# Dealing a kernel's first filter work anew between two engines, and giving its output rows four places in place of two

## The chip, the cores and the metric

The kernel runs on one core of one Trainium2 chip. The metric is the device time of one execution in microseconds (us), lower is better. TensorE does matrix products and transposes, VectorE (DVE), ScalarE (ACT) and GpSimd (POOL) work elementwise, SyncE (SP) asks for transfers, and 16 DMA engines carry them. SP, ACT and POOL each have a queue in which their requests for transfers stand among their other instructions.

## The reference, cut to what matters

Everything is float32. N = 128 samples, C = 32 channels, L = 512 positions.

```python
# block 0
h = conv1d(x, conv_w, 9 taps, pad 4, 4 channel groups of 8)      # (N, 32, 512)
h = h + (cond @ ctx_w.T)[:, :, None] + fside[None, :, None]
top2 = top_k(h @ W_gate + b_gate, 2)                              # 8 experts, per row of 512
x = x + mean over the two chosen experts of relu(h @ W_e + b_e)
# block 1
att = softmax(mlp(cond)); agg_w = att @ mix_w; agg_b = att @ mix_b   # per sample a 32x32 mix
y = agg_w @ x + agg_b
x = x + (y @ dequant(qweight, scales, zeros) + bias)
```

## The kernel before, in words

A group is 4 samples with 32 channels, that is 128 rows of 512; there are NG = 32 groups. The program has three stages, each engine's order is written out by hand, and semaphores tie them.

*Stage 1, convolution and routing (to about 145 us).* The convolution is computed on four interleaved phases of the positions (position = 4 l + q). `split_phase` (L387) copies phase q of a group from the loaded x (32 channels on 32 partitions) to the partitions of `phases`. For each group TensorE does 12 products against the filter `wconv` (L1281), ACT brings the result to `hT` (L598), and gating and ranks follow. For group 0 something must come first: the filter. The weights `conv_w` come in four transfers, one for each channel group, into a zeroed square `wfull`; `pick_taps` (L377) copies 12 shifted pieces of it to `wsel`, three steps t of four pieces p; TensorE turns each step's four pieces (L1205), and DVE copies each step's result to `wconv` (L764). DVE takes two pieces of each step, ACT the other two. ACT asks for two of the four weight transfers and for `bg_bc`, loads its table at its first copy (L589), takes its pieces, and only then copies phases 3 and half of 2 of group 0. DVE takes its pieces, then phases 0 and 1, then the filter copies, then the other half of phase 2. TensorE runs 24 transposes of `ident` ahead of all this (`warm_up`, L1197), whose results nobody reads, and after the filter transposes two small ones for the condition (L1209, L1210), which await `cond_sb` and `cw_sb` from SP's queue.

*Stage 2, expert products (to about 385 us).* 71 blocks of 128 rows are gathered, multiplied by their expert's weights (L1307), and scattered.

*Stage 3, mixing and the last linear layer (from about 385 us).* SP's `load_group(a)` brings x and the pair of expert results of group a; POOL adds (L578), DVE finishes y (L1124, `finish_y`). TensorE goes by pairs of groups a, a+1: `mix_group` (L1351) and `sum_terms` (L1358) of both, `add_terms` of a-1 (L1380), `linear` of both, first with the `high` part (L1368), then the `low` part (L1372), then `add_terms` of a. ACT makes `high` (L711) and `token_rows` (L705), DVE makes `low` (L1108) and scales (L1096, `scale_bank`); `add_terms(c)` waits for `scale_bank(c)`. DVE's `out_row(d)` (L1118) adds y to the finished bank into one of two places `orow[:, d % 2]`, and for that waits until the store of row d-2 has landed (`out_out[d % 2]`). ACT asks for that store in `store_row(d)` (L716), which waits for `out_row(d)`; what stands behind it on ACT waits too. `ring_a` is two tiles of 128x512 that stage 2 uses between DVE and ACT and stage 3 does not.

## Time and profile before

| | us |
|---|---|
| median of 3 runs | 491.54 |
| lowest, highest | 491.21, 492.26 |
| profiled execution, its own time | 496.68 |
| its span in the trace | 494.9 |
| TensorE busy in the span | 480.5 |
| mean granted TensorE clock | 0.992 |

The profiled execution is one of its own and is 5.14 us above the median of the timed ones; 1.8 us of it lie outside the span. The trace gives for each instruction a start, a duration, and what its engine last waited for. A granted clock of 1.00 stands for 2.4 GHz, 0.50 for 1.2 GHz.

### The profile page before, as it was taken

How to read it: one execution, taken by the hardware profiler on the slowest of the kernel's cores; microseconds unless marked ns; L12 is line 12 of the kernel's file. 1: busy time of each engine (PE TensorE's matmuls, PEld its weight loads, DVE VectorE, ACT ScalarE, POOL GpSimd, SP SyncE). 2: the span in 40 equal slices, each digit the busy share in tenths (PEclk: the TensorE clock that was granted, in tenths of full speed). 3: DMA queues.
4: the chain of work that ended last, by engine and by line, in shares of the span. 5: the costliest groups of instructions: out<-in, count | busy, mean ns of one | idle time of the engine just before them, and what ended most of it. 6: DMA issues, size and time to landing. Idle time of an engine off the chain costs nothing.

```text
span 494.9 us, 10081 instructions
## 1 busy us (share of the span) xinstructions
PE 480.5 (97%) x2341; PEld 324.7 (66%) x2342; DVE 323.8 (65%) x966; ACT 176.8 (36%) x309; POOL 196.9 (40%) x215
## 2 busy tenths in 40 slices
PE   7999999999999999999999999999999989999996
PEld 6999999998964444444444444444445667888885
DVE  5688778988747567564354535344356688888885
ACT  5587878898721211111212112112222212211221
POOL 8055555654637532332332323323224434334420
PEclk8899999999999999999999999999999999999999
DMA  6799978998976875777656657576657599999812
GB/s 169 214 330 291 306 235 303 299 295 237 285 195 204 228 220 139 183 219 206 198 154 165 189 151 206 139 201 159 194 151 198 168 368 353 319 312 313 299 72 101
DMA packets 90052, 110.95 MB, mean 224 GB/s; under 512 B 25199, under 2 KB 61727, under 8 KB 88981
## 3 DMA queue, kind: packets, MB, share of 16 engines
q1 hardware_dynamic: 66912, 59.70, 44.4%
q0 software_dynamic: 11952, 37.28, 21.0%
q10 hardware_dynamic: 11144, 13.48, 8.1%
q8 instruction: 16, 0.26, 0.2%
q14 instruction: 28, 0.22, 0.1%
HBM read 65.44 MB, written 46.51 MB: 226 GB/s over the span
## 4 chain that ended last, share of the span: by engine, by line
PE 78%; DVE 9%; issue 4%; DMA 3%; SPq 2%; ACT 1%; DVEq 1%; ACTq 1%; another core or an unknown queue 0%
PE bank L1307 40%; PE bank L1281 14%; PE bank L1268 7%; PE bank L1351 4%; PE bank L1368 4%; PE bank L1372 4%; DMA out<-orow_list 3%; PE bank L1380 2%; PE bank L1358 1%; SPq L454 1%; DVE ring_a L1000 1%; DMA keys<-lists_d 1%; DVE bank L1096 1%; DVE orow_list L1118 1%; DVE phases L387 1%
## 5 line engine op out<-in xcount | busy, mean ns | idle before, releaser
L1307 PE MATMUL bank<-we,lT 128*128 x536 | 232.3, 594 | 0.6 <-DVE ring_a L1000 0.6
L1307 PEld LDWEIGHTS bank<-we,lT 128*128 128x128 f32 x536 | 101.1, 190 | 127.2 <-issue 126.9
L562 POOL DMA_INDIRECT pairs_d<-ring_b,pair_i x71 | 71.5, 1007 | 150.6 <-DVE pair_i L989 99.2
L658 ACT ACTIVATE ring_b<-ring_a 128x512 f32<-128x512 f32 x71 | 44.7, 630 | 191.2 <-DVE ring_a L1000 182.9
L1000 DVE TENSOR_TENSOR ring_a<-bank,be_bc 128x512 f32<-128x512 f32 x71 | 49.1, 692 | 96.9 <-PE bank L1307 50.3
L543 POOL DMA_INDIRECT lists_d<-token_list,row_i x64 | 69.3, 1083 | 72.4 <-issue 33.6
L1281 PE MATMUL bank<-wconv,phases 128*128 128x128 f32 x768 | 93.8, 280 | 0.8 <-ACT phases L387 0.8
L1281 PEld LDWEIGHTS bank<-wconv,phases 128*128 128x128 f32 x768 | 90.8, 196 | 1.7 <-ACT phases L387 1.0
L387 DVE COPY phases<-xt 32x512 f32<-32x512 f32 (+1 forms) x96 | 52.5, 547 | 9.2 <-PE bank L1281 6.0
L387 ACT COPY phases<-xt 32x512 f32<-32x512 f32 x64 | 56.4, 882 | 1.5
L578 POOL TENSOR_TENSOR we<-xt,we 128x512 f32<-128x512 f32 x26 | 33.5, 1291 | 55.7 <-DVE we L1124 49.7
L986 DVE STREAM_TRANSPOSE lT<-xt 128x512 f32<-128x512 f32 x67 | 47.2, 704 | 9.8 <-DMA keys<-lists_d 9.1
L711 ACT CAST high<-bank 128x512 fp32r<-128x512 f32 x32 | 18.6, 584 | 75.9 <-PE bank L1351 72.2
L1268 PE MATMUL bank<-wg,lT 128*128 128x136 f32 x256 | 37.4, 289 | 0.4 <-ACT token_list L622 0.4
L1372 PE MATMUL bank<-wq,low 128*128 128x512 f32 x128 | 35.0, 395 | 1.0 <-DVE low L1108 0.9
L1368 PE MATMUL bank<-wq,high 128*128 128x512 f32 x128 | 35.3, 398 | 0.0
L1268 PEld LDWEIGHTS bank<-wg,lT 128*128 128x128 f32 x256 | 31.8, 190 | 1.3 <-issue 1.2
L1096 DVE TENSOR_TENSOR bank<-bank,scale_bc 128x512 f32<-128x512 f32 x32 | 22.3, 697 | 10.7 <-PE bank L1372 10.5
L1372 PEld LDWEIGHTS bank<-wq,low 128*128 128x128 f32 x128 | 23.8, 188 | 7.7 <-DVE low L1108 2.3
L1368 PEld LDWEIGHTS bank<-wq,high 128*128 128x128 f32 x128 | 24.1, 189 | 5.0 <-issue 0.2
L1351 PEld LDWEIGHTS bank<-mix_bd,we 128*128 128x128 f32 x208 | 25.2, 192 | 1.2 <-DVE we L1124 0.3
L598 ACT COPY lT<-bank 128x512 f32<-128x512 f32 x32 | 18.7, 584 | 20.0 <-PE bank L1281 13.6
(212 smaller groups left out, 379.8 us busy)
## 6 DMA issues: line engine op xcount, KB each, us to landing
xt<-lists_d SPq DMA_DIRECT2D x268, 64.0 KB
xt<-in_x SPq DMA_DIRECT2D x58, 256.0 KB, 4.7
we<-pairs_d SPq DMA_DIRECT2D x26, 512.0 KB, 5.7
we<-in_L_ffn_W_e SPq DMA_DIRECT2D x8, 1024.0 KB
out<-orow_list ACTq DMA_DIRECT2D x32, 256.0 KB, 4.6
words<-pairs_d POOLq DMA_DIRECT2D x6, 512.0 KB, 5.3
lists_d<-orow_list SPq DMA_DIRECT2D x8, 257.0 KB
be_bc<-in_L_ffn_b_e ACTq DMA_DIRECT2D x4, 512.0 KB
```

Source lines behind the costliest of these rows:

```text
L387: return copy(phases[q * C:(q + 1) * C, jb, samples, 1:P + 1], x_quad[jq].rearrange("c s (l q) -> c q s l", q=PH)[:, q, samples, :])
L543: pool.indirect_dma_start(lists_d, bass.IndirectOffsetOnAxis(ap=row_i[:, j, k:k + 1], axis=0), token_list[:, j, :], None, bounds_check=E * ...
L562: pool.indirect_dma_start(pairs_d, bass.IndirectOffsetOnAxis(ap=pair_i[:, s % DR:s % DR + 1], axis=0), ring_b[:, s % U, :], None, bounds_c ...
L658: act.activation(ring_b[:, j, :], ring_a[:, j % 2, :], ACT.Relu, scale=0.5).then_inc(result_ready, 1)
L986: dve.transpose(lT[:, ja, :].rearrange("m (p h r) -> m h p r", p=PH, h=MH), list_of(a, ja).rearrange("r (h p l) -> r h p l", h=MH, p=PH)). ...
L1000: dve.tensor_tensor(ring_a[:, j % 2, :], ps_exp[j % 2][:, :], be_bc[:, bass.ds(expert, 1), :].rearrange("p a n -> p (a n)"), ALU.add).then ...
L1268: mm = pe.matmul(gate_out[:, p, 0:E + P], hT[:, ja % 2, p * P:(p + 1) * P], wg[:, p, :], start=True, stop=True)
L1281: mm = pe.matmul(ps_conv[j % 2][:, s * P:(s + 1) * P], phases[:, j % 2, s, t:t + P], wconv[:, t, :, :].rearrange("k p o -> k (p o)"), star ...
L1307: mm = pe.matmul(ps_exp[j % 2][:, :], lT[:, j, p * P:(p + 1) * P], we[:, bass.ds(expert, 1), p, :].rearrange("m a n -> m (a n)"), start=(p ...
L1351: mm = pe.matmul(ps_mix[a % 2][:, q * P:(q + 1) * P], y_of(a)[:, q * P:(q + 1) * P], mix_bd[:, a, :], start=True, stop=True)
L1368: pe.matmul(ps_lin[j][:, :], high[:, j % 2, q * P:(q + 1) * P], wq[:, q, :], start=(q == 0), stop=False, skip_group_check=True)
L1372: mm = pe.matmul(ps_lin[j][:, :], low[:, j % 2, q * P:(q + 1) * P], wq[:, q, :], start=False, stop=(q == PH - 1), skip_group_check=True)
```

## The change

Three edits.

1. *Start.* SP asks for three weight transfers in place of two, ACT for one; `bg_bc` is asked for after ACT's pieces. DVE takes 8 pieces and ACT 4. DVE copies phases 0 and 1 of group 0 ahead of its pieces and the whole of phase 2 behind them; ACT copies phase 3 ahead of its pieces and nothing of phase 2.
2. *TensorE.* 20 transposes of `warm_up` in place of 24, and 2 behind each step of filter transposes.
3. *End.* `row_ring` has four places, two in `orow` and the two tiles of `ring_a`; `out_row(d)` waits for the store of row d-4. ACT asks for the store of an odd row one step later, between the next pair's two `high_part`.

```diff
+        row_ring = [orow[:, 0, :], orow[:, 1, :], ring_a[:, 0, :], ring_a[:, 1, :]]
...
-        out_out = [sem(f"out_out{i}") for i in range(2)]
+        out_out = [sem(f"out_out{i}") for i in range(U)]
...
+        taps_of_dve = [range(3), range(3), range(2)]
+        taps_of_act = [range(3, PH), range(3, PH), range(2, PH)]
...
-            for s in range(2):
+            for s in range(3):
...
-            for s in range(2, C // CG):
-                rows = slice(s * CG, (s + 1) * CG)
-                act.dma_start(wfull[rows, rows, PH - 1:PH - 1 + TAPS], conv_w[rows]).then_inc(convw_in, 16)
-            act.dma_start(bg_bc[:, :], b_gate.rearrange("(a e) -> a e", a=1).to_broadcast((P, E))).then_inc(bg_in, 16)
+            rows = slice(3 * CG, 4 * CG)
+            act.dma_start(wfull[rows, rows, PH - 1:PH - 1 + TAPS], conv_w[rows]).then_inc(convw_in, 16)
             act.wait_ge(ident_ready, 2)
             act.copy(g0[:, 0:1], ident[:, 0:1])
+            act.wait_ge(pads_ready, 2)
+            act.wait_ge(x_in[0], 16)
+            split_phase(act.copy, 3, 0, 0).then_inc(act_split, 1)
             act.wait_ge(convw_in, 16 * (C // CG))
-            pick_taps(act.copy, range(PH // 2, PH), act_taps)
+            pick_taps(act.copy, taps_of_act, act_taps)
+            act.dma_start(bg_bc[:, :], b_gate.rearrange("(a e) -> a e", a=1).to_broadcast((P, E))).then_inc(bg_in, 16)
...
-                act.dma_start(out_g[g], orow[:, g % 2, :]).then_inc(out_out[g % 2], 16)
+                act.dma_start(out_g[g], row_ring[g % U]).then_inc(out_out[g % U], 16)
...
                 if a > 2:
                     high_part(a)
+                    store_row(a - 3)
                 high_part(a + 1)
                 store_row(a - 2)
                 if a > 2:
                     high_sums(a)
                 high_sums(a + 1)
-                store_row(a - 1)
+            store_row(NG - 3)
...
+            split_x(0, 0)
             dve.wait_ge(convw_in, 16 * (C // CG))
-            pick_taps(dve.tensor_copy, range(PH // 2), dve_taps)
-            split_x(0, 0)
+            pick_taps(dve.tensor_copy, taps_of_dve, dve_taps)
+            split_phase(dve.tensor_copy, 2, 0, 0).then_inc(dve_split, 1)
...
-            split_third(0)
...
-                wait(dve, out_out[d % 2], (d - d % 2) * 8)
-                dve.tensor_tensor(orow[:, d % 2, :], ps_lin[d % U][:, :], y_of(d), ALU.add).then_inc(out_ready, 1)
+                wait(dve, out_out[d % U], (d - d % U) * (16 // U))
+                if d in (2, 3):
+                    dve.wait_ge(result_ready, NT)
+                dve.tensor_tensor(row_ring[d % U], ps_lin[d % U][:, :], y_of(d), ALU.add).then_inc(out_ready, 1)
...
-            warm_up(3 * WARM_START)
+            warm_up(5 * WARM_START // 2)
...
                 mm.then_inc(wT_done, 1)
+                warm_up(2)
```

ACT's first instructions before, up to the copies of group 0 (`words` holds both `wfull` and `wsel`):

```order
L586 DMA words<-in_L_cond_weight 8x8x9 [waits wfull_zero]
L586 DMA words<-in_L_cond_weight 8x8x9
L587 DMA bg_bc<-in_L_ffn_b_gate 128x8
L589 ACT_TABLE_LOAD
L589 COPY g<-ident 128x1 [waits ident_ready]
L377 COPY words<-words 32x128 [waits convw_in]
L377 COPY words<-words 32x128 x5
L387 COPY phases<-xt 32x4x128 [waits x_in0,pads_ready]
L387 COPY phases<-xt 32x2x128
```

And ACT's first instructions now:

```order
L589 DMA words<-in_L_cond_weight 8x8x9 [waits wfull_zero]
L591 ACT_TABLE_LOAD
L591 COPY g<-ident 128x1 [waits ident_ready]
L391 COPY phases<-xt 32x4x128 [waits x_in0,pads_ready]
L381 COPY words<-words 32x128 [waits convw_in]
L381 COPY words<-words 32x128 x3
L597 DMA bg_bc<-in_L_ffn_b_gate 128x8
```

Two requests have left the place ahead of the table load, the phase copy has come ahead of the weights' arrival, and two pieces and the half copy of phase 2 are gone.

DVE's first instructions behind its memset before:

```order
L377 COPY words<-words 32x128 [waits convw_in]
L377 COPY words<-words 32x128 x5
L387 COPY phases<-xt 32x4x128 [waits x_in0]
L387 COPY phases<-xt 32x4x128
L764 COPY wconv<-bank 128x128 [waits wT_done] x3
L387 COPY phases<-xt 32x2x128
```

And the same stretch of DVE now:

```order
L391 COPY phases<-xt 32x4x128 [waits x_in0]
L391 COPY phases<-xt 32x4x128
L381 COPY words<-words 32x128 [waits convw_in]
L381 COPY words<-words 32x128 x7
L391 COPY phases<-xt 32x4x128
L772 COPY wconv<-bank 128x128 [waits wT_done] x3
```

Two phase copies stand ahead of the wait for the weights, and the last one is whole and stands ahead of the filter copies.

ACT in stage 3, from the `high` part of group 3 on, before (L716 is a store):

```order
L711 CAST high<-bank 128x512 [waits lin_done,mixed_done]
L716 DMA out<-orow_list 128x512 [waits out_ready]
L705 CAST rows_r<-bank 34x128 [waits terms_done]
L716 DMA out<-orow_list 128x512 [waits out_ready]
L711 CAST high<-bank 128x512 [waits lin_done,mixed_done] x2
L716 DMA out<-orow_list 128x512 [waits out_ready]
L705 CAST rows_r<-bank 34x128 [waits terms_done] x2
L716 DMA out<-orow_list 128x512 [waits out_ready]
```

The same place on ACT now (L722 is a store):

```order
L717 CAST high<-bank 128x512 [waits lin_done,mixed_done]
L722 DMA out<-orow_list 128x512 [waits out_ready]
L711 CAST rows_r<-bank 34x128 [waits terms_done]
L717 CAST high<-bank 128x512 [waits lin_done,mixed_done]
L722 DMA out<-orow_list 128x512 [waits out_ready]
L717 CAST high<-bank 128x512 [waits lin_done,mixed_done]
L722 DMA out<-ring_a 128x512 [waits out_ready]
L711 CAST rows_r<-bank 34x128 [waits terms_done] x2
```

The store of row 1 stood ahead of the `high` part of group 4 and stands behind it now; rows 2 and 3 of each four leave from `ring_a`.

## Rows read from the trace of the kernel before

**Rows 1.** The page: busy time by engine, and the chain that ended last.
```profile
PE 480.5 (97%) x2341; PEld 324.7 (66%) x2342; DVE 323.8 (65%) x966; ACT 176.8 (36%) x309; POOL 196.9 (40%) x215
...
PE 78%; DVE 9%; issue 4%; DMA 3%; SPq 2%; ACT 1%; DVEq 1%; ACTq 1%; another core or an unknown queue 0%
```

**Rows 2.** The chain that ended last, 0 to 40 us: start, duration, what.
```profile
4.28 1.28 ACT L589
...
5.67 2.01 ACT words L377 x6
...
7.70 1.11 ACT phases L387
...
8.82 0.64 ACT phases L387
...
9.51 5.49 PE bank L1281 x24
...
16.39 2.78 PE bank L1281 x24
```

**Rows 3.** Instructions in order of time, 0 to 30 us: start, duration, instruction.
```profile
3.57 0.43 SPq L401 DMA_DIRECT2D cw_sb<-in_L_cond_c_weight  x1
...
5.26 1.47 DVE L377 COPY words<-words 32x128 f32<-32x128 f32 x6 [3.85 <-DMA words<-in_L_cond_weight]
...
5.58 1.82 SPq L405 DMA_DIRECT2D fs_col<-in_fside_S  x4
...
6.34 1.59 DVE L387 COPY phases<-xt 32x512 f32<-32x512 f32 x2
...
8.15 0.33 PE L1209 MATMUL bank<-ident,cond_sb 128*128 128x128 f32 x1
```

**Rows 4.** Line L1197, to 5.4 us and from 5.5 us: durations in ns, starts.
```profile
L1197 PE MATMUL bank<-ident x18: 357/421/477, 1.6 to 5.3; 128*128 128x128 f32 x18
...
L1197 PE MATMUL bank<-ident x7: 272/273/357, 5.3 to 6.0; 128*128 128x128 f32 x7
```

**Rows 5.** Busy time by stretch; behind the engines clock, DMA share, GB/s.
```profile
5.43:8.86 3.43, 2.49 (x22) 1.84 (x20) 3.37 (x12) 3.38 (x10) 3.43 (x12) 1.00 0.80 201
8.86:15.64 6.78, 6.13 (x29) 6.13 (x29) 2.77 (x7) 2.93 (x4) 3.66 (x7) 0.50 1.05 296
...
397.90:401.30 3.40, 1.69 (x8) 1.07 (x6) 1.55 (x3) 0.00 (x0) 0.00 (x0) 1.00 1.05 413
...
396.00:404.00 8.00, 5.83 (x32) 4.54 (x33) 5.70 (x13) 1.21 (x4) 2.31 (x3) 1.00 1.02 400
```

**Rows 6.** The chain that ended last, from 330 us on.
```profile
393.28 6.38 DMA out<-orow_list
...
423.37 1.78 PE bank L1351 x16
...
430.08 1.78 PE bank L1351 x16
```

**Rows 7.** Instructions in order of time, 372 to 424 us.
```profile
391.64 2.22 PE L1351 MATMUL bank<-mix_bd,phases 128*128 128x128 f32 x16
...
393.73 1.07 ACT L711 CAST high<-bank 128x512 fp32r<-128x512 f32 x2 [3.69 <-DVE orow_list L1118]
...
395.08 0.69 DVE L1118 TENSOR_TENSOR orow_list<-bank,token_list 128x512 f32<-128x512 f32 x1 [1.23 <-DMA out<-orow_list]
...
396.43 1.19 PE L1372 MATMUL bank<-wq,low 128*128 128x512 f32 x4 [0.66 <-DVE low L1108]
...
399.75 0.69 DVE L1118 TENSOR_TENSOR orow_list<-bank,token_list 128x512 f32<-128x512 f32 x1 [2.26 <-DMA out<-orow_list]
...
401.20 0.47 PE L1380 MATMUL bank<-terms_w,rows_r 70*128 70x512 f32 x1 [1.71 <-DVE bank L1096]
...
401.71 2.05 PE L1351 MATMUL bank<-mix_bd,we 128*128 128x128 f32 x16
...
423.20 1.05 PE L1351 MATMUL bank<-mix_bd,we 128*128 128x128 f32 x8
```

More of the change, by code:

```diff
@@ L370, in x_count @@
             return 16 * ((a - PRIMED) // XR + 1)
+        taps_of_dve = [range(3), range(3), range(2)]
+        taps_of_act = [range(3, PH), range(3, PH), range(2, PH)]
         def pick_taps(copy, phases_of, taps_ready):
             for t in range(SHIFTS):
-                for p in phases_of:
+                for p in phases_of[t]:
                     k0 = PH * t - p + PH - 1
@@ L489, in _ @@
             for s in out_out:
-                sp.wait_ge(s, 16 * (NG // 2))
+                sp.wait_ge(s, 16 * (NG // U))
         @block.gpsimd
@@ L600, in step1 @@
                 a = g + 2
-                if live(a, NG):
+                first = isinstance(g, int) and a == 0
+                if live(a, NG) and not first:
                     ja = (j + 2) % U
@@ L625, in step1 @@
                 a = g + 2
-                if live(a, NG):
+                if live(a, NG) and not first:
                     split_phase(act.copy, 2, (j + 2) % U, j % 2, for_act).then_inc(act_split, 1)
@@ L644, in step1 @@
                         act.activation(att_x[:, :], att[:, :], ACT.Exp, accum_out=att_s[:, 0:1]).then_inc(mlp_ev, 1)
-            act.wait_ge(pads_ready, 2)
             stepped(act, step1, -2, lo1, hi1, NG + 2)
```

## The prediction

> **What bounds the kernel now.** I read the page first: TensorE is busy 97% of the span and holds 78% of the chain that ended last [rows 1]. So only two kinds of change can pay: what shortens the time before TensorE's first useful product, or what takes away a stretch in which it waits or runs slowly. The chain in order of time shows where these are.
>
> At the start the chain runs along ACT: its table load, its six filter pieces, the copies of phase 3 and half of phase 2, and then the first convolution at 9.51 [rows 2]. That convolution takes 5.49 us, the next one 2.78 for the same 24 records [rows 2]. The stretches say why: the granted clock is 0.50 from 8.86 to 15.64, with 6.13 us of TensorE work in it, after a stretch in which the engine was busy 2.49 of 3.43 us, and that with small transposes for the most part [rows 5]. At full clock the same work would take half: the low clock costs 6.13 / 2 = 3.07 us. The durations of the warm-up tell one thing more. They fall from 421 to 272 ns at about 5.4 us [rows 4], though the page's clock stands at 1.00 from the start; I take it that TensorE began low, rose 3.85 us after its first transpose (5.43 - 1.58; the warm-up's first start is rounded to 1.6 in the row), fell at 8.86 and rose again at 15.64.
>
> The third stage is bound by TensorE once it has settled: from 423.37 to 430.08 a pair of groups takes 6.71 us [rows 6]. It has not settled at first. The pair that starts at 391.64 takes 10.07 us (to 401.71), and the next three take 21.49 us together (to 423.20) where three settled ones take 20.13 [rows 7]. That is 3.36 + 1.36 = 4.72 us over. The chain names the cause of the larger part: the store of row 1, 6.38 us long [rows 6]. DVE waited 1.23 us for the store of row 0 and 2.26 us for that of row 1; TensorE then waited 0.66 us for the low part and 1.71 us for the scaled bank [rows 7].
>
> **The start, part by part.** *ACT.* Of its two weight transfers one goes, and the one for `bg_bc` moves behind. The table load began at 4.28; it can begin when the first request ends. I put that at 3.05 (the two weight requests together ran from 1.45 to 3.75, and the first of them was the long one), so the load ends at 4.35 instead of 5.56. The phase copy (1.11) then runs from about 4.45 to 5.56. It needs group 0's x. That transfer is asked for first, on the same queue as the weights, which landed at 5.26 [rows 3]; I take it as landed by 4.4. The pieces need the weights, and these come as late as before: the last request leaves SP at about the time when the last left ACT. Four pieces at 2.01 / 6 = 0.335 us end at 6.90. ACT had the last word at 9.46; now it is done at 6.90.
>
> *DVE.* Two phase copies of 0.80 us each (1.59 / 2) [rows 3] fit between x and 5.26 if x has landed by 3.66; if x is late by a, DVE is late by a. Eight pieces at (6.34 - 5.26) / 6 = 0.18 us run to 6.70, the whole copy of phase 2 to 7.50, and only the last filter copy remains, short beside what TensorE does meanwhile.
>
> *TensorE.* Step 0 can be turned at about 6.1 (ACT's first piece ends at 5.97), step 2 after 6.93. Four small transposes take about 0.45 us with their gaps, two fillers at full clock about 0.11 us each, since the warm-up's seven last begin between 5.3 and 6.0 [rows 4]. Steps 0, 1, 2 and their fillers end near 7.8. The condition's two transposes follow. Their data comes from SP behind one more weight request of some 0.7 us: cw_sb was asked for at 3.57 and TensorE got to it at 8.15 without a wait of its own [rows 3]. I put them at 8.0 to 8.5 and the first convolution at 8.5, against 9.51: **1.0 us**. Bounds: 0.4, if the fillers run at low clock (0.21 us each, 6 x 0.1 more) or x makes DVE late by as much; 1.4, if the condition's data is no later than before. The fs_col requests (1.82 us in all) and three loads of x move back by the same 0.7 us; they are covered, since DVE used fs_col at 16.36 and x of group 1 lay there at 9.59. bg_bc is used at 18.0, 11 us after its new place.
>
> *The clock.* Unknown, with bounds 0 and 3.07 us. For a clock that stays up: from 5.43 to 8.86 TensorE would have three warm-ups, six full fillers, the same small transposes and 0.36 us of convolution, some 3.1 of 3.4 us busy; and a stretch of 3.40 us in which the engine was busy only 1.69 us kept 1.00 at 397.90 [rows 5]. Against it: those 1.69 us were large products, most of the new ones are small transposes, and the 2.49 of 3.43 busy at 5.43 did not hold it. I take the clock as kept, 3.0 us, a little nearer to the row at 397.90 than to that at 5.43. The second convolution would start at 8.5 + 6.88 - 3.07 = 12.3 in place of 16.39; its phases need DVE until about 10.8 (two copies for the condition, then 0.6 + 0.6 + 0.4), so nothing new stops it.
>
> The Trainium skill's page "TensorE: Matmul & The Clock Gate", part 1, says of the clock that "the default state is throttled, and activity releases the throttle". The durations at L1197 agree. The advice at the page's end names long idle gaps as what brings the low clock back; the longest gap ahead of the first convolution was under 1 us here and the clock fell all the same, so where page and trace differ the trace decides, and the page alone, which would keep the clock now, is no ground for more than the chance given below.
>
> **The end, part by part.** With four places `out_row(2)` and `out_row(3)` wait for no store, and `out_row(4)` waits for the store of row 0, asked for 10 us earlier; the page gives 4.6 us to landing as the median, and 6.38 is the longest [rows 6]. The store of an odd row, asked for a step later, is awaited a whole pair after that, some 9 us. The new wait for `result_ready` is long met. DVE from 393.16: scale 0.69, out_row(2) to 394.5, low of 4 and 5 (1.28) to 395.8, which needs high of 4. ACT made that at 393.73 because it stood in the store of row 1 [rows 7]; with the store behind it, it is made at about 392.9. Then sums 0.48, out_row(3) to 396.9, scale(4) to 397.6, y of 6 and 7 to 398.9. TensorE has low(4) when it wants it (395.6), scale(4) before 398.4, and begins the next pair at 398.65 in place of 401.71: 3.06 us. The other 1.36 go too if nothing else is late: **4.4 us** in the profiled execution. The ends: 2.4 (0.66 + 1.71 alone) and 4.72. The timed runs are 5.14 us shorter than the profiled one; some of the stores' delay may belong to it alone, so I take **3.9**. The extra request between the two `high` parts costs ACT 0.34 us a pair; ACT idles 5 us a pair. At the very end the last row's store follows its out_row as before: nothing.
>
> **Sum.** 1.0 + 3.0 + 3.9 = 7.9; 491.54 - 7.9 = 483.6.
>
> **Rivals.** *The clock falls, but returns sooner.* The first rise came 3.85 us after the engine got busy; from 8.5 on it is busy without a gap, so a rise near 12.3 is likely where 15.64 was. Low from 8.86 to 12.3 costs 1.7 in place of 3.07: gain 1.4. Sum 1.0 + 1.4 + 3.9 = 6.3: 485.2.
>
> *The clock does as before*, low for 6.78 us from 8.86 with TensorE busy all of it: 3.39 lost, 0.3 more than before. 1.0 - 0.3 + 3.9 = 4.6: 486.9.
>
> *The stores' wait turns into one for loads.* DMA is full between 396 and 404 (share 1.02, 400 GB/s) [rows 5]. If y of 8 to 11 then comes late, TensorE waits where DVE waited, and the tail gives 1.0: 483.6 + 2.9 = 486.5, or 488.1 with the second case of the clock. Against it: a pair needs two loads of 256 KB, two of 512 KB and two stores of 256 KB, 2.1 MB in 6.71 us or 313 GB/s, below the 400 shown. The skill's page "DMA: Bandwidth & Descriptors", in "Issuing engines are not separate DMA queues", says that all requests end on the same 16 engines and interleave: by that alone more stores in flight add no rate, and the tail's gain would be this rival's.
>
> *Slower.* The shorter warm-up ends about 0.4 us after the clock's first rise. Should the rise be missed, and the mix of small transposes and gaps hold it low past the first convolutions, each us of TensorE work costs 0.5 us. It takes 5 us of gain (1.0 - 0.1 + 3.9, about) to be eaten: low for 10 us longer than before, to 25.7. With a low clock to 30 the time would be 493.7. Only one rise is delayed by that, and dense work raised it before; little speaks for it.
>
> **How the numbers follow.** Clock kept 0.42; returns sooner 0.22; as before 0.18; loads in place of stores 0.12; low clock for long 0.06, of which half ends slower. The first gives 483.6, with 482.4 to 485.0 by its own bounds. Range: 482.2 (upper bounds at the start and in the tail) to 487.4 (the third case with a tail of 3.4, and most of the fourth). About 0.2% (1 us) is what a measurement tells from no change: faster 0.94, within it 0.03, slower 0.03.
>
> **What the new profile would show.** The first convolution (now L1291) starts at 8.5 and its 24 records take 2.7 to 2.8 us (kept), or about 5.4 (not), with a clock row of 0.50 only in the latter; ACT ends its pieces by 6.9. DVE's L1127 has no wait for a store. ACT's high of group 4 has no wait for L1127, TensorE's L1390 none of 1.7 us, and pairs follow each other every 6.7 us from the second on. It would be wrong if x of group 0 lands after 5 us, if L1127 or POOL's add waits for transfers in the third stage, or if the clock is low past 12.3.

## The result and the profile after

The changed kernel takes 487.57 us, the median of 7 runs (486.25 to 489.20), against 492.26 for the kernel before, timed beside it (7 runs, 491.21 to 493.15). The ratio is 0.9902, with a 95% interval of 0.9881 to 0.9924: 4.7 us faster, where 7.9 were forecast. The profiled execution took 486.77, with a span of 485.0.

The page of the changed kernel, busy time by engine and the chain that ended last:

```profile
PE 476.7 (98%) x2343; PEld 323.4 (67%) x2344; DVE 324.2 (67%) x968; ACT 175.5 (36%) x306; POOL 197.9 (41%) x215
...
PE 88%; DVE 5%; issue 2%; SPq 2%; DMA 1%; ACT 1%; DVEq 0%; ACTq 0%
```

DMA had 3% of the chain and DVE 9% in [rows 1]; now they have 1% and 5%, and TensorE has 88% where it had 78%. The chain at the start, in order of time:

```profile
4.55 0.82 ACT phases L391
...
5.69 0.42 ACT words L381
...
6.25 0.41 PE bank L1214 x4
6.65 0.37 PE bank L1206 x2
7.02 0.36 PE bank L1214 x4
7.38 0.37 PE bank L1206 x2
7.75 0.36 PE bank L1214 x4
8.11 0.37 PE bank L1206 x2
8.48 0.20 PE bank L1219
...
8.91 4.26 PE bank L1291 x24
...
14.19 2.78 PE bank L1291 x24
```

The part that ran along ACT until 9.5 [rows 2] is gone. TensorE goes from step to step by itself, and its own small work is now what the start consists of: each pair of fillers (L1206) takes 0.37 us of the path. The first convolution starts at 8.91 in place of 9.51 and takes 4.26 in place of 5.49. The clock behind it, in the stretches of [rows 5] (the second cut in two):

```profile
5.43:8.86 3.43, 2.79 (x23) 1.87 (x21) 2.64 (x11) 2.45 (x6) 3.36 (x17) 0.93 0.69 192
8.86:12.27 3.41, 3.41 (x19) 3.41 (x19) 2.09 (x5) 0.88 (x2) 3.41 (x7) 0.57 0.86 215
12.27:15.64 3.37, 3.37 (x33) 3.37 (x32) 2.20 (x6) 2.35 (x3) 0.67 (x2) 1.00 1.03 345
```

It still fell, and came back before 12.27 instead of at 15.64. From the first convolution to the second it is now 5.28 us where it was 6.88, so the clock gave 1.6 us here and not 3.0. That is the rival "the clock falls, but returns sooner", in this execution.

In the third stage, from the timeline:

```profile
387.02 0.59 ACT L717 CAST high<-bank 128x512 fp32r<-128x512 f32 x1 [4.21 <-PE bank L1361]
...
387.32 0.68 DVE L1127 TENSOR_TENSOR ring_a<-bank,token_list 128x512 f32<-128x512 f32 x1
...
389.77 0.69 DVE L1127 TENSOR_TENSOR ring_a<-bank,token_list 128x512 f32<-128x512 f32 x1
...
396.63 1.28 POOL L582 TENSOR_TENSOR we<-xt,we 128x512 f32<-128x512 f32 x1 [2.24 <-DMA we<-pairs_d]
...
399.40 0.47 PE L1390 MATMUL bank<-terms_w,rows_r 70*128 70x512 f32 x1
```

Neither `out_row` carries a wait for a store (1.23 and 2.26 us in [rows 7]), ACT's `high` waits for TensorE alone, and `add_terms` has lost its 1.71 us. POOL does wait for a load, 2.24 us, as the third rival said it might. The chain shows how far apart the pairs start:

```profile
386.10 1.78 PE bank L1361 x16
392.81 1.79 PE bank L1361 x16
399.87 1.78 PE bank L1361 x16
406.77 1.78 PE bank L1361 x16
413.48 1.78 PE bank L1361 x16
```

The pairs follow each other after 6.71, 7.06, 6.90 and 6.71 us. That is 0.35 + 0.19 = 0.54 us over settled pairs. The waits for loads cost at most that here, against the 2.9 that the rival asked for.

### The profile page after: what moved, and what is told of

Its sections match the earlier page's. It is cut to its first block, busy times and chain, and to the rows that moved or that the text cites. A ratio compares the mean times of both kernels' runs of the same rounds, so it can differ in the third digit from the quotient of the medians.

```text
span 485.0 us, 10085 instructions
## 1 busy us (share of the span) xinstructions
PE 476.7 (98%) x2343; PEld 323.4 (67%) x2344; DVE 324.2 (67%) x968; ACT 175.5 (36%) x306; POOL 197.9 (41%) x215
## 4 chain that ended last, share of the span: by engine, by line
PE 88%; DVE 5%; issue 2%; SPq 2%; DMA 1%; ACT 1%; DVEq 0%; ACTq 0%
PE bank L1317 42%; PE bank L1291 16%; PE bank L1378 6%; PE bank L1382 6%; PE bank L1361 6%; PE bank L1278 6%; PE bank L1390 2%; PE bank L1368 2%; SPq L458 1%; DVE phases L391 1%; DMA keys<-lists_d 1%; DVE lT L993 1%; DVE ring_a L1007 0%; ACTq L589 0%; ACT phases L391 0%
## 5 line engine op out<-in xcount | busy, mean ns | idle before, releaser
L1291 PE MATMUL bank<-wconv,phases 128*128 128x128 f32 x768 | 92.7, 278 | 0.0
L1291 PEld LDWEIGHTS bank<-wconv,phases 128*128 128x128 f32 x768 | 89.8, 194 | 0.9 <-issue 0.8
L391 ACT COPY phases<-xt 32x512 f32<-32x512 f32 (+1 forms) x63 | 55.9, 888 | 2.4 <-DMA xt<-in_x 1.0
```

The costliest lines, as they stand in the source:

```text
L391: return copy(phases[q * C:(q + 1) * C, jb, samples, 1:P + 1], x_quad[jq].rearrange("c s (l q) -> c q s l", q=PH)[:, q, samples, :])
L1291: mm = pe.matmul(ps_conv[j % 2][:, s * P:(s + 1) * P], phases[:, j % 2, s, t:t + P], wconv[:, t, :, :].rearrange("k p o -> k (p o)"), star ...
```

## The experiments

There are four sets of runs, each on a chip of its own; every kernel is compared with the kernel before of its set. Times are medians in us. "Clock" counts, of all executions of a kernel, those whose mean granted clock was 0.998 or more, those between, and those of 0.989 or less. At 0.998 or more the clock fell nowhere ahead of the last few us: e12's trace, whose one fall lasted 3.4 us, has 0.996. A lower mean does not say where the clock fell. e11's trace has 0.996 too, but there the clock held at the start and fell at 138 us. So where the text says that so many executions kept the clock, it means 0.998 or more, and counts no execution that kept it at the start and lost it later.

| kernel | time | before in its set | ratio, 95% interval | clock |
|---|---|---|---|---|
| e1 before again | 494.65 | 494.77 | 0.9996 [0.9973, 1.0019] | 0 / 8 / 4 |
| e2 start (edits 1, 2) | 494.55 | 494.77 | 0.9990 [0.9961, 1.0018] | 0 / 10 / 2 |
| e3 end (edit 3) | 489.69 | 494.77 | 0.9877 [0.9839, 0.9915] | 1 / 5 / 0 |
| e4 changed | 488.62 | 494.77 | 0.9877 [0.9844, 0.9910] | 4 / 2 / 0 |
| e5 four places, stores as before | 490.08 | 495.69 | 0.9874 [0.9846, 0.9903] | 2 / 3 / 1 |
| e6 two places, later stores | 510.21 | 495.69 | 1.0292 [1.0261, 1.0324] | 0 / 0 / 6 |
| e7 changed, no fillers | 487.76 | 495.69 | 0.9839 [0.9816, 0.9862] | 5 / 0 / 0 |
| e8 edits 2 and 3 | 488.81 | 495.69 | 0.9860 [0.9837, 0.9884] | 2 / 4 / 1 |
| e9 no fillers, x first | 486.41 | 494.42 | 0.9850 [0.9810, 0.9890] | 4 / 2 / 0 |
| e10 edit 3, x first | 489.96 | 494.42 | 0.9914 [0.9882, 0.9946] | 2 / 4 / 0 |
| e11 as e7 | 488.01 | 494.42 | 0.9870 [0.9829, 0.9910] | 3 / 3 / 0 |
| e12 changed | 488.81 | 494.42 | 0.9894 [0.9861, 0.9926] | 4 / 2 / 0 |
| e13 changed, x first | 488.70 | 495.58 | 0.9864 [0.9837, 0.9890] | 2 / 4 / 0 |
| e14 as e9 | 486.07 | 495.58 | 0.9810 [0.9780, 0.9839] | 5 / 1 / 0 |
| e15 changed | 488.22 | 495.58 | 0.9851 [0.9816, 0.9886] | 3 / 3 / 0 |

Marks from their traces: when the durations of TensorE's first transposes drop (421 to 272 ns for the warm-up's, as in [rows 4]; a drop behind the warm-up is read from the filter's) and whether the clock then fell at the start or was kept; the starts of the first two convolutions and of the first gating product, the time from there to that of the last group, the start of the third stage's first pair, and the next four pairs together (four settled ones take 26.84).

| profiled execution | drop, clock | conv(0) | conv(1) | first gating | to the last | first pair | four pairs | span |
|---|---|---|---|---|---|---|---|---|
| before | 5.4, fell | 9.51 | 16.39 | 19.01 | 122.64 | 391.64 | 31.56 | 494.9 |
| e1 before | 5.0, fell | 9.49 | 16.16 | 18.77 | 120.60 | 389.35 | 31.23 | 492.6 |
| e2 start | 5.1, fell | 8.88 | 14.22 | 16.84 | 121.22 | 387.12 | 32.61 | 491.5 |
| e3 end | 4.9, fell | 9.48 | 16.11 | 18.73 | 120.49 | 389.34 | 27.23 | 488.5 |
| after | 5.0, fell | 8.91 | 14.19 | 16.81 | 119.48 | 385.93 | 27.39 | 485.0 |
| e4 changed | 6.5, kept | 8.87 | 12.76 | 15.38 | 121.42 | 386.44 | 27.21 | 485.6 |
| e12 changed | 5.2, fell | 8.77 | 14.24 | 16.85 | 121.35 | 387.62 | 26.88 | 486.4 |
| e15 changed | 4.4, fell | 9.32 | 15.77 | 18.39 | 120.90 | 388.19 | 27.19 | 487.3 |
| e11 no fillers | 4.6, kept | 8.16 | 12.09 | 14.71 | 123.00 | 387.88 | 26.96 | 486.8 |
| e9 no fillers, x first | 5.8, kept | 8.42 | 12.35 | 14.97 | 121.17 | 385.32 | 27.16 | 484.2 |
| e14 as e9 | 6.6, kept | 8.44 | 12.37 | 14.99 | 121.64 | 385.55 | 26.96 | 484.4 |
| e13 fillers, x first | 6.4, kept | 8.81 | 12.71 | 15.32 | 121.89 | 386.81 | 27.31 | 486.1 |
| e5 four places | 4.7, fell | 9.52 | 16.02 | 18.64 | 121.30 | 391.68 | 27.29 | 490.9 |
| e6 two places, later stores | 5.7, fell | 9.52 | 14.88 | 17.50 | 120.17 | 388.03 | 38.02 | 507.9 |
| e7 no fillers | 4.4, kept | 8.47 | 12.26 | 15.02 | 122.26 | 386.89 | 27.29 | 486.1 |
| e8 edits 2 and 3 | 5.4, fell | 9.51 | 16.38 | 18.99 | 122.10 | 392.61 | 27.22 | 491.8 |
| e10 edit 3, x first | 7.5, kept | 9.50 | 13.46 | 16.08 | 122.31 | 388.46 | 26.85 | 487.0 |

The first column orders most of the outcomes. In the ten traces whose clock fell the durations drop between 4.4 and 5.7 us. In five of the seven that kept it they drop at 5.8 or later, whatever the edits: e10 has the old start. The other two, e7 and e11, drop early and kept it all the same; both run without fillers. What moves the drop from one execution to the next the traces do not show.

### First set: the two halves apart

**e1** is the kernel before without an edit.

> The kernel before, unchanged, to see how its executions differ among themselves and what its spans look like in other profiled executions. Theory A (the recorded execution of 496.68 us was an outlier, and part of its stall at the stores of rows 0 and 1 belongs to it alone): this profile has a span near 490 us, the pair of groups 4 and 5 takes clearly less than 10.07 us, and out_row(0) has no wait of 2.4 us. Theory B (the stall is typical and the gain was lost elsewhere in the changed kernel): a span near 490 us too, but with the pair still at about 10 us and a shorter start or middle.

Its trace differs from the first one by 2.3 us of span (492.6 and 494.9), 2.04 of them between the first and the last gating product. The stall is there too: the pair of groups 4 and 5 takes 10.17 us (389.35 to 399.52) where the first trace had 10.07, and behind it stand the same two waits:

```profile
DVE orow_list L1118 <- DMA out<-orow_list: 3.2, 2, 2.6
...
PE bank L1380 <- DVE bank L1096: 2.1, 1, 2.1
```

So theory B holds, the stall is typical. Over the four sets the kernel before ran 68 times, from 491.94 to 498.23.

**e2** has the start alone:

```diff
-            pick_taps(act.copy, range(PH // 2, PH), act_taps)
+            pick_taps(act.copy, taps_of_act, act_taps)
...
-            warm_up(3 * WARM_START)
+            warm_up(5 * WARM_START // 2)
...
                 mm.then_inc(wT_done, 1)
+                warm_up(2)
```

> Edits 1 and 2 alone (the new deal at the start, the fillers), with the old two places at the end. Theory A: the start is worth what the trace of the changed kernel shows, 2.2 us (16.39 to 14.19 at the second convolution), so 2.2 us faster than before, 1.5 to 3. Theory B: the clock takes most of it back in the median execution, 0.7 us faster. My prediction on record had 4.0.

It measured 494.55, against 494.65 for e1: nothing that can be told from no change, though its profiled execution is 1.94 us ahead of e1's at the second convolution and 2.23 ahead at the first pair. In the third stage it gives 1.38 back, four pairs taking 32.61 us where e1's take 31.23. From its timeline:

```profile
396.05 0.69 DVE L1123 TENSOR_TENSOR orow_list<-bank,token_list 128x512 f32<-128x512 f32 x1 [4.85 <-DMA out<-orow_list]
...
397.49 0.68 PE L1386 MATMUL bank<-terms_w,rows_r 70*128 70x512 f32 x1 [3.73 <-DVE bank L1101]
```

With two places the store of row 0 (7.63 us long here) holds the second pair up just as before. The stall costs more than its length, as the stretches behind it show:

```profile
397.00:398.00 1.00, 0.51 (x2) 0.21 (x2) 1.00 (x4) 0.00 (x0) 0.00 (x0) 0.79 1.02 406
398.00:399.00 1.00, 1.00 (x5) 1.00 (x5) 1.00 (x3) 0.00 (x0) 0.83 (x1) 0.50 1.07 430
```

After 3.73 us without work TensorE's clock was 0.50 from 397.6 to 401, and 3.4 us of its time went at half speed. In [rows 5] the clock had stayed up in a stretch with waits of 1.71 us and less, so I had not counted this. It stayed up behind e1's wait of 2.05 us as well.

**e3** has the end alone:

```diff
-        out_out = [sem(f"out_out{i}") for i in range(2)]
+        out_out = [sem(f"out_out{i}") for i in range(U)]
...
-                wait(dve, out_out[d % 2], (d - d % 2) * 8)
+                wait(dve, out_out[d % U], (d - d % U) * (16 // U))
...
+                    store_row(a - 3)
...
-                store_row(a - 1)
```

> Edit 3 alone (four row places, each odd store a step later), with the old start. Theory A: 2.5 us faster than before, since the typical stall is smaller than the recorded one. Theory B: 3.9 us, as predicted.

5.1 us faster. Four pairs take 27.23 us, 4.00 less than e1's. The rest of the 5.1 may be a second fall of the clock, argued from counts and not shown: of the 68 executions of the kernel before, 31 had a mean clock of 0.989 or less (median 496.03, the others' 494.3), and of the 25 of the changed kernel none had. But neither trace of the kernel before has such a fall, and four places do not rule a second fall out, as e5 and e8 show below.

**e4** is the changed kernel again.

> The changed kernel again, beside its parts on the same chip. Theory A and B: 4.7 us faster than before. If the parts add, e2 and e3 sum to it within 0.7 us.

488.62: the start adds 1.1 us to e3, with intervals that overlap. Here the clock was kept: the first convolution took 2.88 us and the second started at 12.76, 3.35 ahead of e3's. At the end of the span 2.9 of that is left, though between the medians it is 1.1. In the timeline around the seventh group a load of x is late:

```profile
36.05 1.28 DVE L391 COPY phases<-xt 32x512 f32<-32x512 f32 x2 [1.27 <-DMA xt<-in_x]
```

TensorE then stood idle for 1.05 us, until 39.43.

### Second set: what each edit of the halves does

**e5** has the four places, and each store where it stood.

```diff
+        row_ring = [orow[:, 0, :], orow[:, 1, :], ring_a[:, 0, :], ring_a[:, 1, :]]
...
-                wait(dve, out_out[d % 2], (d - d % 2) * 8)
+                wait(dve, out_out[d % U], (d - d % U) * (16 // U))
```

> Half of edit 3 on the kernel before: four row places, but each store asked for where it was. Theory A (the wait for a row place makes the stall): out_row(2) and out_row(3) wait for no store; ACT still stands in the store of row 1, so high of group 4 is made some 0.8 us late and TensorE may wait 0.2 to 0.6 us for the low part. 4.5 us faster than before, the granted clock never at 0.98 to 0.99 for want of a second fall. Theory B (the place of the store request on ACT matters as much): 2 to 3 us faster.

5.6 us faster, as much as e3, and its four pairs take 27.29 us where e3's take 27.23. The later request adds nothing that can be measured. One part of the expectation failed: the profiled execution had a mean clock of 0.988. Its clock fell a second time, but not in the third stage: TensorE waited 1.03 us ahead of the last group's gating products, and from 141.2 to 144.6 us the clock was 0.50.

**e6** is the opposite: two places, and the later request.

```diff
                     high_part(a)
+                    store_row(a - 3)
...
-                store_row(a - 1)
+            store_row(NG - 3)
```

> The other half of edit 3 alone: each odd row's store asked for a step later, with the old two places. Theory A: high of group 4 comes earlier, but out_row(3) now waits for a store of row 1 asked for later, by about 0.4 us, and the same in each later pair, so no faster than before and up to 1 us slower. Theory B: 1 to 2 us faster.

It is 14.5 us slower, far outside what I expected. The waits of its third stage up to 480 us (us in total, times, longest):

```profile
DVE orow_list L1119 <- DMA out<-orow_list: 22.2, 12, 4.0
...
PE bank L1381 <- DVE bank L1097: 13.3, 6, 3.5
```

With two places `out_row(d)` needs the store of row d-2, and the edit asks for that of an odd row later. So the wait that [rows 7] show at two rows comes at twelve, and more than half of its time reaches TensorE. TensorE's clock also fell three times there, at 398, 419 and 443 us. The places carry the whole gain, and the later request is harmless only because of them.

**e7** is the changed kernel without the fillers.

```diff
-            warm_up(5 * WARM_START // 2)
+            warm_up(3 * WARM_START)
...
                 mm.then_inc(wT_done, 1)
-                warm_up(2)
```

> The changed kernel without edit 2: 24 transposes ahead and none between the filter steps. Theory A (fillers raise the clock at the start): the first convolution starts at about 8.3 instead of 8.9, at low clock for about 6 us, the second starts near 15.0; 1 to 2 us slower than the changed kernel, mean clock 0.99. Theory C (the fillers cost on TensorE's path what they give in clock): the same time as the changed kernel within 0.5 us.

487.76, about as fast as the changed kernel (theory C), and the clock was kept in all five executions, where theory A had it low. The stretches of its trace:

```profile
5.43:8.86 3.43, 2.31 (x21) 1.76 (x19) 3.34 (x14) 2.82 (x7) 3.43 (x16) 1.00 0.63 183
8.86:15.64 6.78, 6.78 (x63) 6.78 (x62) 5.26 (x13) 3.30 (x5) 3.99 (x8) 1.00 0.92 270
```

TensorE was busy 2.31 of 3.43 us ahead of a clock that held; in [rows 5] it was busy 2.49, and with the fillers 2.79, ahead of one that fell. So the fillers were not needed to keep the clock. But then a load of x is late. The chain, and the copies that wait:

```profile
9.82 10.95 DMA xt<-in_x
```

```profile
20.79 1.13 ACT L391 COPY phases<-xt 32x512 f32<-32x512 f32 x1 [1.38 <-DMA xt<-in_x]
20.85 1.25 DVE L391 COPY phases<-xt 32x512 f32<-32x512 f32 x2 [2.37 <-DMA xt<-in_x]
```

The load asked for at 9.82 landed 10.95 us later. SP asks for the first expert's weights (1 MB) and a list head right ahead of it. TensorE stood idle for 0.93 us behind that, at 23 us.

**e8** has the end and the fillers, with the filter work dealt as before.

```diff
-            warm_up(3 * WARM_START)
+            warm_up(5 * WARM_START // 2)
...
                 mm.then_inc(wT_done, 1)
+                warm_up(2)
```

> Edits 2 and 3 without edit 1: old deal of the filter pieces, 20 transposes ahead and two behind each step. Theory A: the convolution starts at 9.5 as before, the clock falls less often or comes back sooner; 0.5 to 1.5 us faster than the end alone (489.7), so near 488.7. Theory C: the clock falls as before, because the gap ahead of the first convolution stays, and the time is that of the end alone.

488.81, 1.3 us under e5 with intervals that overlap widely. Its profiled execution had the first convolution at 9.51 and the second at 16.38, as in [rows 2]: there the fillers did nothing for the clock. It took 493.53, the slowest of the seven, and had the same second fall as e5's, from 141.9 to 145.3 us behind a wait of 1.08 us.

### Third set: x ahead of the experts' weights

**e9** takes e7 and lets SP ask for an expert's weights and list head behind two loads of x, where they stood ahead of four.

```diff
             sp.wait_ge(consts, N_CONSTS)
-            load_we(0)
-            zero_head(0)
...
                     sp.dma_start(x_quad[j], x_sub[bass.ds(k * XR + XR + j, 1)].rearrange("a c s l -> c (a s) l")).then_inc(x_in[j], 16)
-                load_we(k + 1)
-                zero_head(k + 1)
+                    if j == 1:
+                        load_we(k)
+                        zero_head(k)
+            load_we(E - 1)
+            zero_head(E - 1)
```

> The changed kernel without edit 2, and in SP's queue each 1 MB load of an expert's weights (with its 257 KB of list heads) is asked for behind two loads of x instead of ahead of four. Theory D (an earlier start runs into the loads of x that were asked for at 9.8 us behind the first expert's weights; DVE waited 2.4 us for them): DVE has no wait for x at 20 us, the interval of 4.89 us between gates becomes 3.8, and it is 1.1 to 2 us faster than the changed kernel without edit 2, so about 486. Theory E (the load's rate is the limit, its place in the queue is not): the same time within 0.5 us, the wait only moves.

486.41, the fastest of its set and 1.6 us under e11, which differs from it by the order of the loads alone; their intervals overlap. What e7's engines waited for `xt` up to 45 us:

```profile
DMA xt<-in_x: 7.2, 5
```

and e9's, of which 2.3 are DVE's wait for the very first load:

```profile
DMA xt<-in_x: 3.0, 2
```

**e10** is the control, the same order of loads with edit 3 and the old start.

```diff
-            load_we(0)
-            zero_head(0)
...
+                    if j == 1:
+                        load_we(k)
+                        zero_head(k)
```

> The same move of the expert loads on the kernel with edit 3 alone, where the start is the old, late one. Theory D: nothing waited for x there, so no difference to edit 3 alone (5.1 us faster than the kernel before) within 0.5 us. Theory E: the same.

489.96, no better than e3 or e5 against their own kernels before (ratios 0.9914, 0.9877, 0.9874, overlapping). The order of the loads brings nothing that can be measured to a kernel that starts late. Its trace shows something else. The start is the old one, without fillers, and yet the clock was kept:

```profile
9.50 2.94 PE bank L1286 x24
...
13.46 2.78 PE bank L1286 x24
```

The second convolution starts 2.65 us ahead of e3's, and ahead of the changed kernel's 14.19. The warm-up shows the difference to [rows 4], where the last seven are short; here no transpose of the 24 is:

```profile
L1202 PE MATMUL bank<-ident x24: 420/421/476, 1.6 to 6.5; 128*128 128x128 f32 x24
```

So a clock kept at the start does not need edit 1 or edit 2. It does not need the new order of loads either: e3 and e5, with the old one, kept it in 3 of 12 executions. Of all executions with four places, 7 of 25 with the old start kept it (e3, e5, e8, e10) and 32 of 54 with the new one. The new start may make it likelier, but that was not tested apart.

**e11** is e7 again, and **e12** the changed kernel.

> The changed kernel without edit 2 again, beside the changed kernel on the same chip. In the first look it was 7.9 us faster than before where the changed kernel, on another chip, was 6.2. Theory C (the fillers cost what they give): 0 to 0.7 us faster than the changed kernel. Theory A (the fillers hold the clock): 1 us or more slower.

> The changed kernel beside the three above, for the comparison on one chip: 5 to 6 us faster than before, and its span less that of e11 shows what the fillers cost.

488.01 and 488.81: without the fillers the kernel is 0.8 us faster here and e7 0.9 faster than e4 (two sets), inside the intervals each time. e11's trace has the late fall that e5's and e8's have, behind a wait of 1.00 us:

```profile
137.70:141.20 3.50, 3.49 (x10) 2.61 (x11) 1.47 (x7) 0.88 (x2) 1.96 (x2) 0.51 0.81 179
```

### Fourth set: does a kept clock reach the end?

**e13** is the changed kernel with e9's order of loads, fillers and all.

```diff
-            load_we(0)
-            zero_head(0)
...
+                    if j == 1:
+                        load_we(k)
+                        zero_head(k)
```

> The changed kernel whole, with its fillers, and each expert load and list head asked for behind two loads of x instead of in front of four. Theory A (a clock kept at the start gives its time back to x loads that come too late): with the loads out of the way the executions with a mean clock of 0.998 or more are 2.5 to 3.5 us faster than those of 0.996 or less, where the changed kernel's own 19 executions so far show no difference (medians 488.4 and 488.2), and the median is 1.5 to 2.5 us under the changed kernel's, near 486.5. Theory B (the order of the loads is worth nothing by itself, the third call's lead was the missing fillers): within 0.7 us of the changed kernel of this call. In the trace no copy of phases waits for x between 9 and 45 us by A.

**e14** is e9 again, without fillers.

> The best kernel of the third call again: the changed kernel without fillers, 24 warm-up transposes, the same order of loads. If fillers cost what they take on TensorE's path (conv(0) 0.4 us later) and the clock holds as often without them: 0.4 us under the kernel with fillers. If the fillers keep the clock up in more executions, this one is 0 to 1 us slower than it and shows fewer executions at 0.998 or more. Against the kernel before: 1.2 to 1.8% faster.

**e15** is the changed kernel a fourth time.

> The changed kernel as it is, for this call. 1.0 to 1.3% faster than the kernel before. Theory A: no difference, or under 1 us, between its executions with the clock at 0.998 or more and the others; more than half of them at 0.998 or more, of the kernel before almost none. Theory B expects 2.5 to 3.5 us between the two kinds.

e13 measured 488.70, no better than e15's 488.22; e14 measured 486.07, 9.5 us faster than the kernel before. So theory A fell in the form that I gave it: no copy waits for x in e13's trace after 9 us, and it is not faster. Both together, x first and no fillers, are 2.4 us under the changed kernel in the third set (e9, e12) and 2.1 in the fourth (e14, e15). Of the two, the part of the fillers stands out of the noise and that of the loads (e9 against e11, e13 against e15) does not. e13's and e14's intervals of the ratio ([0.9837, 0.9890] and [0.9780, 0.9839]) overlap by 0.0002, and only one execution of e14 (488.08) is slower than e13's fastest (487.81). Of the 2.6 us between them, 0.37 are the later first convolution; e14 kept the clock in 5 of 6 executions and e13 in 2.

Over all executions of a kernel, the median with the clock at 0.998 or more against the rest: changed kernel 488.26 (13) and 488.81 (12), so a kept clock went with half a us; e9 and e14 485.93 (9) and 488.69 (3), so there with 2.8. These numbers mix chips, and they are small. Within a set the difference was 0.2, 0.9, 0.2 and 2.1 us for the changed kernel (after, e4, e12, e15), 0.3 for e13, 3.6 and 2.1 for e9 and e14, and 2.4 for e11, which has the old order of loads. The old start shows the same: 0.1 with fillers (e8), 2.0 and 1.9 without (e5, e10). So a kept clock mostly pays where there are no fillers, whatever the order of the loads. e15 is the exception; its 2.1 comes close to theory B, and 3 of its 6 executions kept the clock where theory A wanted more than half.

What a fall amid the fillers costs is in e15's chain:

```profile
7.39 0.37 PE bank L1206 x2
7.76 0.48 PE bank L1214 x4
8.24 0.62 PE bank L1206 x2
```

At the low clock the last pair takes 0.62, and the first convolution starts at 9.32, not 8.91.

## Why the prediction came out as it did

**The end was right, and a little small.** The step was 3.9 us, 4.4 in the trace. The traces show 4.00 (e1 to e3), the timed runs 5.1 (e3) and 5.6 (e5). The chain of causes stood as written: no wait at L1127, `high` of group 4 early, `add_terms` on time. I cut the 4.4 because the profiled execution of the kernel before was 5.14 us above the median and I took part of its stall for its own. That was a wrong reason. Its length was nothing of the profiling: e1's trace, of an execution of 494.32, has the same stall (10.17 us), and executions of this kernel lie between 491.2 and 498.2, the profiled one among them. A term that I left out is the second fall of the clock that a long stall can bring, shown in e2 alone; how much of the 5.1 to 5.6 it is stays open.

**The third rival**, a wait for loads where the stores were, was seen at POOL, and cost at most 0.54 us in four pairs. POOL's wait was one of my signs of being wrong; it came, and the gain stayed. The store's median landing went from 4.6 us to 6.2 in the changed kernel. In e5, which has the four places too, it stayed at 4.8 to 5.0, so more stores in flight alone need not lengthen it. Longer landings agree with what the Trainium skill's page "DMA: Bandwidth & Descriptors" says in "Issuing engines are not separate DMA queues", that all requests run on the same 16 engines and interleave. The conclusion that the tail's gain would go with it did not hold here.

**The start, 1.0 us, gave 0.6** in the traces (9.49 to 8.88 in e2, 9.51 to 8.91 after). ACT was done about as worked out: its pieces ended at 7.04, 6.90 forecast. Mis-sized were "two fillers at full clock about 0.11 us each": a pair takes 0.37 us of the path, 3 x 0.15 = 0.45 more than 3 x 0.22. With a first step at 6.25 in place of 6.1 the three steps ended at 8.48 where I had 7.8; the condition's two transposes then took 0.43 us where I had allowed 0.7, which leaves 8.91 against 8.5. The lower bound named the fillers only for a low clock.

**The clock, 3.0 us, is the step that failed**: "I take the clock as kept, 3.0 us". In the profiled execution it fell, and gave 1.6. Of 25 executions of the changed kernel 13 kept it. Of 68 of the kernel before one did, but these two counts do not compare the starts alone, since a fall anywhere counts; with four places the old start kept it in 7 of 25. So about half the time the clock was kept, but not by the means that I gave, a fuller stretch ahead (I had 3.1 of 3.4 us busy; it was 2.79): e7 kept it without fillers and with less TensorE work in the stretch than before, e10 kept it with the old start, and the traces go mostly by when the warm-up's durations dropped. And keeping it did not bring 3.0. With 5.1 for the end, the 6.15 of e4 leaves 1.1 for start and clock together, where I had 4.0. The second convolution came 2.2 us sooner in the profiled execution after and 3.4 sooner in e4, yet the timed runs have the start at 0.1 us alone (e2 against e1) and 1.1 on top of the end (e4 against e3). Two places where time is given back are shown: at the stores when there are only two places (1.4 us in e2), and at late loads of x (waits of DVE of 1.27 us in e4 and 2.37 in e7, of which 1.05 and 0.93 reached TensorE). The second is my sentence "so nothing new stops it". It looked at DVE's copies for the second group and at the loads of the first four, and not at the loads that follow, which SP asks for behind a megabyte of weights. e9 and e14 take that wait away, and there a kept clock goes with 2.8 us. But that does not show the loads to be the cause: e13 has no late load either and a kept clock went with 0.3 us there, and e11 has them and it went with 2.4. Why a kept clock is worth so little with the fillers in place stays open.

**The sum.** With 5.1 for the end and 0.1 to 1.1 for the start the parts give 5.2 to 6.2; the changed kernel itself gave 6.15, 5.6 and 7.4 in e4, e12 and e15. The first result, 4.7, lies below; its kernel before, at 492.26, was faster than in any later set (494.4 to 495.7). The rival "the clock does as before" (4.6) gives its number and the rival "returns sooner" (6.3) its trace.

**Slower** did not happen. The nearest thing is e15's trace, with the clock low from 7.8 to 14.7 us, and that execution took 489.08 all the same.

**Open.** What decides in an execution when the warm-up's durations drop, and with it mostly whether the clock falls at the start; the same kernel does either. Why e13, with no late load and fillers, is 2.6 us behind e14, of which the marks explain 0.37 by the first convolution; the clock's counts explain little, since e13's own executions differ by 0.3 us with it. And what makes the time from the first to the last gating product vary from 119.5 to 123.0 us among the profiled executions: that spread is as large as what the start had to give. The seven traces that kept the clock at the start average 122.0 us there and the ten others 121.0, which may be where some of a kept clock goes.

## What to carry to other kernels

Time won at the start has to be followed past the next step, to every load that later work of that stage needs: compare the time from each request to its landing with the new time of use, and try asking for those loads ahead of bulk ones that nobody wants yet. Here that took the waits away; its own gain, 1.6 us in one set, was within the noise. When a result buffer's stores stall a pipeline, give the ring more places first; asking for a store later without more places made the same kernel 14.5 us slower. Dummy work between real small steps lies on TensorE's path, so try the edit without it before keeping it: here the kernel without it was never slower, and with the loads in order 2.6 us faster. And a gain that hangs on the clock at the start should be forecast as a share of the executions, counted over many of them, and not as a yes or no.

## What the runs showed of the hardware

- TensorE's granted clock at the start differs between executions of one program. The mean clock of the kernel before was 0.982 to 0.998 in 68 executions, and its time 491.9 to 498.2.
- Whether it falls at the start goes mostly with when the warm-up's transposes drop from 421 to 272 ns: between 4.4 and 5.7 us in all ten traces that fell, at 5.8 or later in five of the seven that did not.
- How long TensorE was busy from 5.43 to 8.86 does not settle the outcome: 2.31 and 2.70 of 3.43 us in e7 and e11, which kept the clock, against 2.49 [rows 5] and 2.79 (after), which lost it. The five others that kept it had 2.92 to 3.29, more than any that lost it.
- A wait of TensorE of 3.73 us in the third stage was followed by a clock of 0.50 for 3.4 us (e2); waits of 1.71 [rows 5, 7] and 2.05 us (e1) were not. Late in the first stage waits of 1.00 to 1.08 us were followed by such a fall in e5, e8 and e11, and one of 1.05 us in e15 was not.
- A load of x asked for behind 1 MB of weights landed 10.95 us after its request (e7).
